# Identity products ahead of the transposes of eight normalisations, and 160 streamed columns in four routers and one value product

## The reference

```python
def _layernorm(x, axis=-1, eps=1e-05):
    m = jnp.mean(x, axis=axis, keepdims=True)
    v = jnp.var(x, axis=axis, keepdims=True)
    return (x - m) / jnp.sqrt(v + eps)
...
    # L0_ffn: router with a hidden layer, two of eight experts
    logits = _gelu(x @ w1 + b1) @ w2 + b2
...
    # L1_ffn: router straight from the tokens, one of eight
    route = jax.nn.softmax(hidden_states @ router_w + router_b, axis=2)
...
    # L3_attn: one key and one value head of width 16, shared by 12 heads
    v = (x @ Wv + bv).reshape(b, s, 1, HD)
...
    # L3_attn's mixture: one of eight
    gates = jax.nn.softmax(xt @ Wg + bg, axis=-1)
...
    # L3_ffn: two of eight, with a capacity
    logits = xf.astype(jnp.float32) @ gate_w.T
```

## Time and profile before

| | us |
|---|---|
| median of 3 executions (lowest, highest) | 2860.68 (2859.81, 2863.6) |
| the profiled execution's own time | 2845.84 |
| its span from first to last instruction | 2844.1 |
| PE busy, of the span | 1802.2 (63%) |
| DVE busy, of the span | 1506.8 (53%) |
| ACT busy, of the span | 1097.8 (39%) |
| POOL busy, of the span | 333.3 (12%) |

### The profile page before, as it was taken

How to read it: one execution, slowest core, us unless ns; L and a number is a source line. 1 busy time by engine, 2 the same in 40 slices (tenths; PEclk the granted TensorE clock), 3 DMA queues, 4 the chain that set the end, 5 groups by cost and what they waited for, 6 DMA issues and landing times. The chain is left out here.

```text
span 2844.1 us, 36917 instructions
## 1 busy us (share of the span) xinstructions
PE 1802.2 (63%) x11724; PEld 1508.5 (53%) x11724; DVE 1506.8 (53%) x2878; ACT 1097.8 (39%) x2121; POOL 333.3 (12%) x403
## 2 busy tenths in 40 slices
PE   3798869577012777645995523324966596459993
PEld 2466759366011344524993423222945596359993
DVE  5777741421576999674224599986143202542223
ACT  5455642223023777720112288863332132112220
POOL 0000000057000000001330000000000232013330
PEclk8766869699556888855996755555975698579996
DMA  3100000245200000013661000000020353236674
GB/s 81 52 15 15 20 9 1 56 118 158 70 14 2 6 5 3 2 35 97 190 168 51 3 6 4 5 1 0 1 78 30 86 164 106 75 95 195 194 194 123
DMA packets 149000, 179.94 MB, mean 63 GB/s; under 512 B 40525, under 2 KB 121952, under 8 KB 148829
## 3 DMA queue, kind: packets, MB, share of 16 engines
q1 hardware_dynamic: 122369, 138.15, 17.5%
q0 software_dynamic: 15360, 31.48, 4.1%
q10 hardware_dynamic: 11100, 8.11, 1.0%
HBM read 144.83 MB, written 30.70 MB: 62 GB/s over the span
## 5 line engine op out<-in xcount | busy, mean ns | idle before, releaser
L819 PE MATMUL 55_l3f_mlp_first<-55_l3f_mlp_xT,55_l3f_mlp_w 96*128 96x128 f32 x1632 | 193.0, 277 | 0.0
L819 PEld LDWEIGHTS 55_l3f_mlp_first<-55_l3f_mlp_xT,55_l3f_mlp_w 96*128 96x128 f32 x1632 | 188.8, 194 | 0.0
L878 DVE TENSOR_TENSOR 55_l3f_mlp_hidden<-55_l3f_mlp_gate,55_l3f_mlp_first 128x512 f32<-128x512 f32 x51 | 35.1, 687 | 214.4 <-ACT 55_l3f_mlp_gate L859 214.4
L819 PE MATMUL 32_l1f_mlp_first<-32_l1f_mlp_xT,32_l1f_mlp_w 96*128 96x128 f32 x928 | 110.6, 278 | 0.0
L819 PEld LDWEIGHTS 32_l1f_mlp_first<-32_l1f_mlp_xT,32_l1f_mlp_w 96*128 96x128 f32 x928 | 108.3, 195 | 0.0
L1955 PE MATMUL 20_pla_line<-20_pla_low,ident 128*128 128x435 f32 x96 | 68.1, 876 | 62.0 <-ACT 20_pla_low L2003 62.0
L1100 PE MATMUL 2_performer_p_u<-perf_proj,2_performer_yT 96*87 96x384 f32 x204 | 98.6, 636 | 8.1 <-DVE 2_performer_arg L1262 6.9
L2155 PE MATMUL 36_log_int_turned<-identb,36_log_int_ratio 128*87 128x128 bf16 x272 | 32.7, 315 | 107.3 <-DVE 36_log_int_ratio L2618 107.3
L195 ACT ACT_TABLE_LOAD x11 | 14.1, 1283 | 210.8 <-PEq L905 98.6
L859 ACT ACTIVATE 55_l3f_mlp_gate<-55_l3f_mlp_first 128x512 f32<-128x512 f32 x51 | 30.5, 597 | 149.6 <-PE 55_l3f_mlp_first L819 149.6
L2155 PEld LDWEIGHTS 36_log_int_turned<-identb,36_log_int_ratio 128*87 128x87 bf16 x272 | 29.1, 193 | 108.9 <-DVE 36_log_int_ratio L2618 108.9
(11 more groups left out here) (892 smaller groups left out, 5162.0 us busy)
## 6 DMA issues: line engine op xcount, KB each, us to landing
55_l3f_mlp_w<-in_L_ffn_w_dram SPq DMA_DIRECT2D x102, 384.0 KB, 4.0
32_l1f_mlp_w<-in_L_ffn_w_dram SPq DMA_DIRECT2D x58, 384.0 KB, 4.4
48_l3a_mlp_w<-in_L_attn_W_dram SPq DMA_DIRECT2D x58, 288.0 KB
9_l0f_mlp_w<-in_L_ffn_down_w_dram SPq DMA_DIRECT2D x102, 96.0 KB
l3a_experts_w<-in_L_attn_W_dram SPq DMA_DIRECT2D x8, 576.0 KB, 8.4
20_pla_blocks<-l1a_qkb SPq DMA_DIRECT2D x192, 5.4 KB, 1.8
l1f_experts_w<-in_L_ffn_w_dram SPq DMA_DIRECT2D x8, 384.0 KB, 6.6
36_log_int_blocks<-l2a_qkb SPq DMA_DIRECT2D x192, 5.4 KB, 1.8
```

What stands on the lines that cost most here:

```text
L819: ins = nc.tensor.matmul(first[j % 2][a][:, t // 4, t % 4, :], w1[j % NW][0:n, k, cols:cols + 128], xT[j % 2][0:n, k, :], start=(k == 0), ...
L878: v.tensor_tensor(hidden[j % 2][:], gate[j % 2][:], first[j % 2][1][:, 0, 0:HT, :], ALU.mult).then_inc(hidden_done, 1)
```

## The change

Two things are added. Ahead of its transposes PE makes products of the identity with itself into a PSUM tile that the transposes overwrite: 45 where the stage takes its own statistics, else 9. They wait for nothing. In the four routers and the value product, POOL makes a copy of the weights padded with zeros to 160 columns, PE waits for it, and each product then streams 160 columns instead of 8 (16). The products of a tile write zeros over the places of later tiles, which write theirs afterwards. Nothing is removed.

```diff
@@ norm_stage
+BUSY = 9
+        own = stats is None
...
             @block.tensor
             def _(pe):
+                for n in range(5 * BUSY if own else BUSY):
+                    nc.tensor.matmul(turned[1][:, 0, 0:128], kit.ident[:, 0:KP], kit.ident[:], start=True, stop=True)
                 for i in range(N):
                     pe.wait_ge(normed, i + 1)
@@ router_stage
+STREAM = 160
+        rows = w[0].shape[0]
+        wide = kit.sb(ctx, "wide", [rows, len(w), STREAM])
...
         @block.gpsimd
         def _(pool):
+            nc.gpsimd.memset(wide[:, :, E:STREAM], 0.0).then_inc(widened, 1)
+            for k, ww in enumerate(w):
+                nc.gpsimd.tensor_copy(wide[:, k, 0:E], ww).then_inc(widened, 1)
             nc.gpsimd.iota(rank[:], pattern=[[-1, E]], base=E, channel_multiplier=0,
...
         @block.tensor
         def _(pe):
+            pe.wait_ge(widened, 1 + len(w))
             for b in range(TN):
-                for k, (x, ww) in enumerate(zip(tokens_t, w)):
-                    ins = nc.tensor.matmul(logits[:, b, :], x[:, b * TP:(b + 1) * TP], ww,
+                for k, x in enumerate(tokens_t):
+                    ins = nc.tensor.matmul(p_logits[:, b * E:b * E + STREAM], x[:, b * TP:(b + 1) * TP], wide[:, k, :],
                                            start=(k == 0), stop=(k == len(w) - 1))
             ins.then_inc(logits_done, 1)
@@ l3_attn, stage l3a_values
+            wide = kit.sb(ctx, "wide", [KP, HALVES, STREAM])
+            @block.gpsimd
+            def _(pool):
+                nc.gpsimd.memset(wide[:, :, DH:STREAM], 0.0).then_inc(widened, 1)
+                nc.gpsimd.tensor_copy(wide[:, :, 0:DH], wv[:]).then_inc(widened, 1)
             @block.tensor
             def _(pe):
+                pe.wait_ge(widened, 2)
                 for i in range(TN):
                     for k in range(HALVES):
-                        ins = nc.tensor.matmul(p_v[:, i * DH:(i + 1) * DH], XT[:, k, i * TP:(i + 1) * TP],
-                                               wv[:, k, :], start=(k == 0), stop=(k == 1))
+                        ins = nc.tensor.matmul(p_v[:, i * DH:i * DH + STREAM], XT[:, k, i * TP:(i + 1) * TP],
+                                               wide[:, k, :], start=(k == 0), stop=(k == 1))
                 ins.then_inc(value_done, 1)
```

More of the change, by code:

```diff
@@ L1388, in router_stage @@
         rank = kit.sb(ctx, "rank", [TP, E])
+        rows = w[0].shape[0]
+        wide = kit.sb(ctx, "wide", [rows, len(w), STREAM])
         p_logits = kit.ps(ctx, "logits", [TP, 512])
-        chain, made, logits_done, shifted, exped = (
-            kit.sem(ctx, n) for n in ("chain", "made", "logits_done", "shifted", "exped"))
+        chain, made, widened, logits_done, shifted, exped = (
+            kit.sem(ctx, n) for n in ("chain", "made", "widened", "logits_done", "shifted", "exped"))
         block = ctx.enter_context(nc.Block())
@@ L1599, in l3_attn @@
             v = kit.sb(ctx, "v", [TP, TN, DH])
+            wide = kit.sb(ctx, "wide", [KP, HALVES, STREAM])
             p_v = kit.ps(ctx, "p_v", [TP, 512])
-            value_done, chain = kit.sem(ctx, "value_done"), kit.sem(ctx, "chain")
+            value_done, chain, widened = kit.sem(ctx, "value_done"), kit.sem(ctx, "chain"), kit.sem(ctx, "widened")
             block = ctx.enter_context(nc.Block())
+            @block.gpsimd
+            def _(pool):
+                nc.gpsimd.memset(wide[:, :, DH:STREAM], 0.0).then_inc(widened, 1)
+                nc.gpsimd.tensor_copy(wide[:, :, 0:DH], wv[:]).then_inc(widened, 1)
             @block.tensor
             def _(pe):
+                pe.wait_ge(widened, 2)
                 for i in range(TN):
                     for k in range(HALVES):
-                        ins = nc.tensor.matmul(p_v[:, i * DH:(i + 1) * DH], XT[:, k, i * TP:(i + 1) * TP],
-                                               wv[:, k, :], start=(k == 0), stop=(k == 1))
+                        ins = nc.tensor.matmul(p_v[:, i * DH:i * DH + STREAM], XT[:, k, i * TP:(i + 1) * TP],
+                                               wide[:, k, :], start=(k == 0), stop=(k == 1))
                 ins.then_inc(value_done, 1)
```

## The result

The changed kernel takes 2834.31 us, the median of 5 executions (2833.43 to 2844.09), against 2859.81 us for the kernel before in the same runs (2857.68 to 2863.6). The ratio is 0.9918, 95% interval [0.99, 0.9936]. Two later series, each beside the kernel before, gave 22.1 and 15.4 us for the same change, so the size of the gain in the time is known only to some 10 us.

The account below looks back on a forecast made before the run. Prediction: no engine is busy over 63%, and narrow products keep PE's clock at half. Terms -10.2 - 0.5 - 0.4 - 1.5 = -12.6 us take the profile from 2845.84 to 2833.2; with 14.8 us to the median, 2848, range 2838 to 2862.

Parts of the forecast that it names:

- What bounds the kernel: Whole kernel: no engine busy over 63%; narrow products last as long as their 128-column load, and PE's clock stays at half.
- what a product of 160 columns costs: Padded streams: 0.268 us a product at half instead of 0.21, 0.135 at full instead of 0.11; pays only if the level changes.
- Value product, l3a router, l3f router: Three padded streams: 0.65 us wait, clock full after 5.9 us, 15.4 us against 18.85; -3.4 each, -10.2 us together.
- l1f router: Padded l1f router: DVE's own work until 1301.65 covers PE's earlier end, so only the 0.51 us wait goes: -0.5.
- l0f router: Padded l0f router: starts at full and the dense stream holds it, 6.4 us against 6.9: -0.4; +3.4 if the level falls.
- The moved clearing: Clearing moved ahead of 53_l3f_dispatch: its 1.5 us or so stay on the path in both places, so nothing.
- Bursts of 9: Normalisations without own statistics: burst takes 1.9 us of 3.5 us room, PE then idle 1.6 us; costed at nothing.
- Rival B: Bursts carry the transposes too, all eight normalisations run them at full: another 17 us, or 2831; chance 0.12.
- Bursts of 45: 3_norm, 42_norm, 44_norm: burst lasts 7.1 to 8.1 us within 9.3 us of free PE; 0.5 us gained each, -1.5 together.

## Why the prediction was wrong, point by point

**What bounds the kernel, what a product of 160 columns costs: right.** In the changed kernel's streams passes stand 0.136 us apart at full and 0.267 at half, against 0.135 and 0.268. A narrow product is as long as its load in the earlier trace rows, 18.88 us of PE and 18.84 of PEld for 88 of each; that the load sets this length was my estimate, for the two are alike with 160 columns as well (14.42 and 14.18 us in the value product). What the runs show is the distance of two passes: 0.213 us at half for 8, 16, 64 and 128 columns, and 0.267 for 160.

**Value product, l3a router, l3f router: right, and a little small.** The forecast was 15.4 us each with the wait; measured are 14.42, 14.71 and 14.13 us of PE and some 0.5 us more wait (1.65 us before the value product instead of 1.1). The level rose after 4.5, 5.1 and 3.9 us instead of 5.9, and what ran before has a part in that: in the value product the rise came after 4.5 to 4.7 us in the three profiles with bursts of 45 ahead, after 6.2 with no burst and 160 columns (21.4 us, not 20.6), and after 6.6 with 34. -4.0, -3.6 and -4.2 instead of -3.4 each.

**l1f router: right**, -0.5. DVE goes from its unrelated work into its first operation on the logits without idle time:

```profile
1309.44 0.32 DVE L2685 TENSOR_SCALAR l2a_v_row<-l2a_v_row,l2a_low 96x192 f32<-96x192 f32 x1
1309.79 0.34 DVE L1448 TENSOR_TENSOR 30_l1f_router_p<-30_l1f_router_logits,l1f_b 128x176 f32<-128x176 f32 x1
```

**l0f router: right for the changed kernel** (44 passes in 6.24 us, all at full, in its three profiles), but its -0.4 can't be told, since with the dispatch behind it the two profiles of before differ by 1.1. That a dense stream holds the level doesn't always hold: with streams alone, with bursts of 4 and 22, and with 9 and 34, the clock fell 0.9 to 1.4 us after this router's first product and rose again 3.4 us later, and the stage took 17.8 us instead of 16.1. **The moved clearing: right**; it stands in stage 52 now, and the two stages together lose what the stream loses.

**Bursts of 9: the step that failed.** "The burst takes 1.9 us at half; PE is then idle again for 1.6 us ... so I cost it at nothing." A product of 128 columns was priced as one pass, and it is two. The burst takes 3.8 us at half and fills all of the 3.5 us of room and 0.3 to 0.5 more, and the transposes follow without a gap. The clock rose between 0.4 us before and 1.9 us after the first transpose in 29_norm, 34_norm, 39_norm and 50_norm (nine profiles), and the sparse transposes then kept it. The other half of the step, that a burst so much shorter than the 4.5 us of the earlier trace rows brings nothing, fell with it. Instead of nothing, the five bursts brought 12 to 18 us, with the following stages. Rival B had this mechanism at 0.12, weakened by the pause of 1.6 us that doesn't exist. Its argument from 29_norm, where transposes alone had held 1.00, was right: 34_norm's transposes ran 10.2 us at 1.00 with nothing else on PE. There the burst had raised it; in 29_norm of both profiles of the kernel before it rose 5.8 us after the first transpose with nothing but transposes on PE.

**Bursts of 45: mis-sized by the same term.** Priced at 7.1 to 8.1 us within a room of 9.3, the burst took 11.8 in 42_norm and delayed the first transpose by 2.4, and by 3.1 and 3.0 in 3_norm and 44_norm. What the clock gives these stages was small, as argued: ACT was to bind them, and even the burst of 34, which fits in 42_norm, brought at most 0.7. So +5.3 us for three stages instead of -1.5. One step was 12 to 18 us too poor and the other 6.8 too good, so part of each error was hidden by the other.

**The sum against its own execution.** I took the profile's 2845.84 and kept a difference of 14.8 us to the median. That execution wasn't one of the five timed ones, which begin at 2857.68. 9_l0f_mlp was 144.8 us in it and 172 to 177 in nine later profiles, of before and of others; in the four of the second series, on another chip, it was 145 to 146. This didn't enter the predicted difference, but where such a stage decides, two profiles aren't enough.

**What stays open.** Why the same burst of 6 had the clock in 34_norm and not in 29_norm; whether a burst's length or its nearness to the first transpose counts; what sets the length of 9_l0f_mlp; and where in 2_performer, ahead of every changed instruction, 278 to 304 us come from. The latter goes with its mean clock (0.79 and 0.71 at the ends).

## What to carry to other kernels

Count a matmul's rows in the trace before pricing one: the count beside the calls in the code says how many passes each is. Size a filler burst in passes, and measure its room in the trace. Here the bursts that lasted until the real work began brought the clock every time, those that ended 0.6 us before it two times of four, and what went beyond the room delayed the first transpose by as much. For a stream of narrow products that stays at the half clock with PE busy throughout (here 0.213 us a pass, at 8 columns as at 16), try several widths of padding: here 128 columns brought the clock at no price per pass, 160 cost 0.024 us a pass more at full, and 64 brought nothing.

## What of the hardware was unexpected

- Float32 products of 128 and 160 columns appear as two passes each, of 0.109 (0.112 in the streams) and 0.136 us at full, 0.213 and 0.267 at half; transposes with the identity are one pass.
- 88 passes of 64 columns left the clock at 0.50 for 19.0 us with PE busy throughout; passes of 128 columns at the same distance raised it after 4.0 to 7.0 us. The profile's busy time (PE 19.04 of 19.10 us with 64 columns, 13.39 of 13.50 with 128) doesn't tell these two apart.
- Once up, the level was held by 44 transposes that kept PE busy 7.25 of 10.2 us (34_norm). At half the same transposes left it there for 13.4 us in 50_norm before, but raised it after 5.8 us in 29_norm and, in the second profile of before, after 7.1 us in 39_norm.
- A stage without any changed instruction (9_l0f_mlp) took 145 to 146 us in the series on one chip and 172 to 177 in those on two others. The first profiles of before and of the changed kernel have 144.8 and 176.0; their chips are not on record, so that the chip sets it isn't shown.
